# Shared down projection (last four tiles) and small attention's output projection in three float32r passes

## The chip, the cores and the metric

One core of a Trainium2 chip runs the whole kernel. The metric is device time in microseconds of that core; a kernel's figure is the median of several executions. Five engines work side by side: TensorE (PE) multiplies, its weight loads (PEld) are listed apart, VectorE (DVE), ScalarE (ACT) and GpSimd (POOL) compute on vectors, and SyncE (SP) starts the DMAs. They wait for each other by semaphores that are written out in the program.

## What is computed

Two layers on 1024 tokens of 256 features, in float32. Only the end of the second layer is touched by the change:

```python
# second layer; x: [1024, 256] tokens after its layernorm
attn = einsum('bhqk,bhkd->bhqd', probs, v)      # small attention: 16 heads of 16, over 4 positions
out  = attn @ weight_proj.T                     # [1024, 256] x [256, 256]
...
shared = silu(x @ Wsg) * (x @ Wsu) @ Wsd        # hidden width 704; Wsd: [704, 256]
shared = shared * sigmoid(x @ Wse)
...                                             # 32 experts, 4 for each token, with 32 slots each
out = shared.at[tok].add(y_pair)
x = x + attention_out + ffn_out
```

## The kernel before

The tokens are in 8 tiles of 128 (`NT`), the features in 2 chunks of 128 (`C`). `X` holds the residual, one [128, 256] block per tile. Most matmuls of the kernel are done in **three float32r passes** by `mm3` (L794 to L798): each operand is split into a high part (its copy rounded to float32r) and a low part (what is left, rounded too), and high x low, low x high and high x high are added up in one bank of PSUM. The parts are built by two engines: ACT copies the raw tensor to the high part, DVE subtracts the high part from the raw tensor. Other matmuls are plain float32.

The order of the work is written out by hand, separately for each engine. The end of the program is this:

- TensorE runs the list `EXPERT_STEPS`, in which the experts and the shared up projection take turns. The shared hidden values lie in `ACTT`, six chunks of 128 hidden rows ([128, 1024 tokens] each; the last one partly padding), raw float32. The shared down weights are `SD`, [128, 6, 256], raw, loaded long before.
- `shared_down(j)` (L1174) multiplies token tile j of the six chunks by `SD`, six float32 products of 128x128 by 128x256, into bank j % 4. Tiles 0 to 3 come first, then 16 transposes (L1202) that turn the small attention's output `AO` into banks 4 to 7, then tiles 4 to 7, each of which waits until DVE has added the tile that lay in its bank (`s_x2`).
- ACT copies the four banks of transposed heads into `AOT` (L789).
- The output stage (L1206 to L1218): for each tile, two float32 products of `AOT` with `projT`, the attention's output weights (L1214), and 16 float32r passes that take the experts' outputs `YH` and `YL` to their tokens by the masks `GT` (L1216, L1217), all in bank 4 + j % 4. From tile 4 on it waits until DVE has emptied the bank (`s_pa`).
- DVE builds the last masks (L1588), the eight low parts of the experts' outputs (`y_low`, L1592), then adds the shared tiles into `X`, scaled by the gate (`add_shared`, L1621), then the output tiles (`add_rest`, L1627). ACT builds the eight high parts of the experts' outputs (`y_high`, L758) before its four copies.
- SP stores each tile of `X` when `add_rest` is done.

Of the kernel before, what the change touches and what calls it, by code (L numbers as in the profile page):

```python
# [5 lines left out]
F32 = mybir.dt.float32  # L6
FR = mybir.dt.float32r
BF16 = mybir.dt.bfloat16
U32 = mybir.dt.uint32
ALU = mybir.AluOpType  # L10
ACT = mybir.ActivationFunctionType
AX = mybir.AxisListType.X

P = 128
B, T, D = 4, 256, 256
N = B * T
NT = N // P
C = D // P
# [25 lines left out]
FC = 6  # L44
FT = FS - P * (FC - 1)
SLOTS = E1 * CAP
GR = SLOTS // P
# [6 lines left out]
def program(nc, a, out):  # L54
    ctx = ExitStack()
    with ctx:
        def sb(name, shape, dt=F32):
            return ctx.enter_context(nc.sbuf_tensor(name, shape, dt))

        def sem(name):  # L60
            return ctx.enter_context(nc.semaphore(name))


        pb = [ctx.enter_context(nc.psum_tensor(f"bank{i}", [P, 512], F32)) for i in range(8)]
# [9 lines left out]
        at_xt = nc.sbuf_base  # L74
# [8 lines left out]
        at_wa = nc.sbuf_base  # L83
# [5 lines left out]
        at0 = nc.sbuf_base  # L89
        arena = sb("arena", [P, 35840])  # L90

        def region(at, words):
            return arena[:, at:at + words]
# [35 lines left out]
        projT = sb("projT", [P, C, D])  # L129
# [39 lines left out]
        def up_weights(g, e):  # L169
            parts = WGU[g % PLACES]  # L170
            return parts[e * len(parts) // EPG][:, e % (EPG // len(parts))]

        SGR = region(9728, 4 * FS).rearrange("p (a c n) -> p a c n", a=2, c=C)
        ACTT = [region(12800 + N * m, N) for m in range(3)] + [WAF[:, 0:N], WAF[:, N:2 * N], region(27648, N)]
# [10 lines left out]
                    (6, 0, 4, 0, 6), (7, 0, 2, 4, 6), (7, 2, 4, 0, 7)]  # L185
        SD = FRF[:, 0:1536].rearrange("p (m n) -> p m n", m=FC)
        AOT = XT
        XE = region(28672, 2048).rearrange("p (c n) -> p c n", c=C)
        SC = region(30720, 512).rearrange("p (f i h j) -> p f i h j", f=2, i=4, h=H1)
        SCf = region(30720, 512).rearrange("p (x j) -> p x j", j=4)  # L190
# [83 lines left out]
        s_ps = sem("shared_down_padding_ready")  # L274
        s_sg = sem("shared_up_weights_loaded")
        s_sd = sem("shared_down_weights_loaded")
# [16 lines left out]
        s_sm = sem("shared_product_done")  # L293
# [9 lines left out]
        s_up = sem("expert_up_done")  # L303
# [16 lines left out]
        s_ac = sem("attn1_transposed_copied")  # L320
# [12 lines left out]
        s_gt = sem("slot_masks_ready")  # L333
        s_yr = sem("expert_output_high_ready")
        s_yl = sem("expert_output_low_ready")
        s_fo = sem("attn1_projected")
        s_pa = sem("attn1_added")
        s_out = sem("out_stored")
# [33 lines left out]
        shared = [(0, 0), (1, 0), (0, 1), (1, 1)] + [(m, half) for m in range(2, FC) for half in range(2)]  # L372
# [176 lines left out]
        def _(act):  # L549
# [11 lines left out]
            for f in range(4):  # L561
                half, c = f // 2, f % 2
# [76 lines left out]
            def o_copy(u):  # L639
                _, _, b, h = unit(u)  # L640
                act.wait_ge(s_O, u + 1)
                nc.scalar.activation(QO[:, h, b], pb[4 + u % 2][:, 0:256], ACT.Identity,  # L642
                                     bias=VC[:, 32 + h:33 + h]).then_inc(s_Oc, 1)
# [103 lines left out]
            for half in range(2):  # L747
                act.wait_ge(s_di, NT)
                act.wait_ge(s_sr, 9)
                nc.scalar.activation(XE[:, 0, 512 * half:512 * half + 512], pb[4 + half][:], ACT.Copy).then_inc(s_xe, 1)  # L750
            for half in range(2):
# [4 lines left out]
            def y_high(n):  # L756
                act.wait_ge(s_ye, n + 1)
                nc.scalar.activation(YH[:, n], YE[:, n], ACT.Copy, scale=slot_w[:, n:n + 1]).then_inc(s_yr, 1)  # L758
# [25 lines left out]
                        y_high(i)  # L784
            y_high(6)
            y_high(7)
            for f in range(4):
                act.wait_ge(s_at, f + 1)
                nc.scalar.activation(AOT[:, f // 2, 512 * (f % 2):512 * (f % 2) + 512], pb[4 + f][:], ACT.Copy).then_inc(s_ac, 1)  # L789


        @block.tensor
        def _(pe):
# [92 lines left out]
            for c in range(C):  # L886
                for o in range(3):
                    ins = pe.transpose(pb[5 + c][:, P * o:P * o + P], stQKV[:, o, P * c:P * c + P], ident[:])
# [207 lines left out]
            for j in range(NT):  # L1096
                for i in range(j + 1):
                    ins = pe.matmul(pb[6][:, E1 * j:E1 * j + E1], (trib if i == j else onesb)[:], selb[:, i],
                                    start=(i == 0), stop=(i == j))
# [38 lines left out]
            def expert_up(g):  # L1138
# [8 lines left out]
                for c in range(C):  # L1147
                    for e in range(EPG):
                        s = slice(CAP * (EPG * g + e), CAP * (EPG * g + e) + CAP)
                        ins = pe.matmul(pb[4 + g % 2][CAP * e:CAP * e + CAP, 0:2 * F1], XE[:, c, s], up_weights(g, e)[:, c],  # L1150
                                        start=(c == 0), stop=(c == C - 1), skip_group_check=True)
# [22 lines left out]
            def shared_down(j):  # L1174
                if j >= 4:
                    pe.wait_ge(s_x2, j - 3)
                for m in range(FC):
                    ins = pe.matmul(pb[j % 4][:, 0:D], ACTT[m][:, P * j:P * j + P], SD[:, m], start=(m == 0), stop=(m == FC - 1))  # L1178
                ins.then_inc(s_sh, 1)

            for what, n in EXPERT_STEPS:
# [13 lines left out]
            for j in range(4):  # L1195
                shared_down(j)
            pe.wait_ge(s_ye, GR)
            pe.wait_ge(s_pv, 32)
            for f in range(4):
                c, half = f // 2, f % 2  # L1200
                for i in range(4):
                    ins = pe.transpose(pb[4 + f][:, P * i:P * i + P], AO[:, 4 * half + i, P * c:P * c + P], ident[:])  # L1202
                ins.then_inc(s_at, 1)
            for j in range(4, NT):
                shared_down(j)
            pe.wait_ge(s_ac, 4)  # L1206
            pe.wait_ge(s_gt, GR)
            pe.wait_ge(s_yl, GR)
            for j in range(NT):
                if j >= 4:  # L1210
                    pe.wait_ge(s_pa, j - 3)
                dst = pb[4 + j % 4][:, 0:D]
                for c in range(C):
                    pe.matmul(dst, AOT[:, c, P * j:P * j + P], projT[:, c], start=(c == 0), stop=False)  # L1214
                for g in range(GR):
                    pe.matmul(dst, GT[:, g, P * j:P * j + P], YH[:, g], start=False, stop=False)  # L1216
                    ins = pe.matmul(dst, GT[:, g, P * j:P * j + P], YL[:, g], start=False, stop=(g == GR - 1))  # L1217
                ins.then_inc(s_fo, 1)  # L1218
# [3 lines left out]
        def _(dve):  # L1222
# [89 lines left out]
            def chosen(k):  # L1312
                return (iota[:, None, 0:E0].to_broadcast([P, NT, E0]), topf[:, :, k:k + 1].to_broadcast([P, NT, E0]))

            for g in range(4):
# [17 lines left out]
                if g == 2:  # L1333
# [6 lines left out]
                    for k in range(2):  # L1340
                        i, t = chosen(k)
                        dst = coef if k == 0 else tmpk
# [159 lines left out]
            def shared_product(q):  # L1502
                m, half = shared[q]
                dst = ACTT[m][:, 512 * half:512 * half + 512]
                dve.wait_ge(s_ss, q + 1)
                dve.wait_ge(s_sf, 2 * q + 2)
                if m == FC - 1:
                    nc.vector.tensor_tensor(dst[P - FT:P], dst[P - FT:P], pb[up_bank(q)][P - FT:P], ALU.mult).then_inc(s_sm, 1)
                    return
                nc.vector.tensor_tensor(dst, dst, pb[up_bank(q) + 1][:], ALU.mult).then_inc(s_sm, 1)  # L1510
# [54 lines left out]
            for half in range(2):  # L1565
                dve.wait_ge(s_di, NT)
                nc.vector.tensor_copy(XE[:, 1, 512 * half:512 * half + 512], pb[6 + half][:]).then_inc(s_xd, 1)
            shared_product(3)
# [21 lines left out]
            def y_low(n):  # L1590
                dve.wait_ge(s_yr, n + 1)
                nc.vector.scalar_tensor_tensor(out=YL[:, n], in0=YE[:, n], scalar=slot_w[:, n:n + 1], in1=YH[:, n].bitcast(F32),  # L1592
                                               op0=ALU.mult, op1=ALU.subtract).then_inc(s_yl, 1)
# [25 lines left out]
            def add_shared(j):  # L1619
                dve.wait_ge(s_sh, j + 1)  # L1620
                nc.vector.scalar_tensor_tensor(out=X[:, j], in0=pb[j % 4][:, 0:D], scalar=sig[:, j:j + 1], in1=X[:, j],  # L1621
                                               op0=ALU.mult, op1=ALU.add).then_inc(s_x2, 1)
# [7 lines left out]
            slot_mask(7)  # L1630
            for n in range(GR):
                y_low(n)
            for j in range(NT):
                add_shared(j)
            for j in range(NT):
                add_rest(j)
# [23 lines left out]
```

## Time and profile before

| | |
|---|---|
| median of 3 executions | 476.18 us (475.53, 476.18, 476.19) |
| the profiled execution's own time | 475.46 us |
| its span | 473.7 us |
| PE busy | 452.1 us (95%) |
| PEld busy | 386.8 us |
| DVE busy | 287.5 us (61%) |
| ACT busy | 212.6 us (45%) |
| POOL busy | 59.9 us (13%) |

The span is the profiled time from the first instruction to the last; the execution's own time also takes in what lies around it, 1.8 us here. Busy time counts overlapping instructions once. Matmuls are pipelined, so the time from one start to the next is what a matmul costs, and its own duration is longer. A float32 product is recorded as two matmuls and two weight loads, a float32r pass as one of each.

### The profile page before, as it was taken

To read this page: it belongs to the slowest core of one execution; us is meant where nothing else is said; L and a number is where in the kernel's file an instruction comes from. 1 tells how busy PE (TensorE), PEld (TensorE's weight loads), DVE (VectorE), ACT (ScalarE), POOL (GpSimd) and SP (SyncE) were. 2 spreads that over 40 slices of the span, in tenths; PEclk is the share of its full clock that TensorE was granted. 3 is DMA by queue.
4 is the path that set the end of the run, shared out by engine and by line. 5 is a ranking of instruction groups with operands and counts; after the bars stand their busy time and mean duration, and the time that the engine had idled before them with its cause. 6 is when DMAs were issued, how large, how long until landed. Compare 5 with 4: busy or idle time off the path is not lost.

```text
span 473.7 us, 8069 instructions
## 1 busy us (share of the span) xinstructions
PE 452.1 (95%) x2934; PEld 386.8 (82%) x2934; DVE 287.5 (61%) x851; ACT 212.6 (45%) x554; POOL 59.9 (13%) x94
## 2 busy tenths in 40 slices
PE   2999999899999999999999989999998999999997
PEld 2788888698998989898989779999986755658897
DVE  5646564667676766667666555667789953545111
ACT  3454730356566566566555777233253052232000
POOL 3050000000000000000000000011345269600000
PEclk9999999999999999999999999999999999999999
DMA  6900510101000010100000000000499369910011
GB/s 202 237 28 1 178 64 26 45 1 41 5 20 27 1 46 1 46 1 0 2 1 1 1 1 1 1 1 0 172 301 292 94 166 291 309 29 2 0 46 44
DMA packets 40439, 32.32 MB, mean 68 GB/s; under 512 B 6432, under 2 KB 38864, under 8 KB 40400
## 3 DMA queue, kind: packets, MB, share of 16 engines
q1 hardware_dynamic: 40400, 31.80, 24.0%
q8 instruction: 24, 0.39, 0.3%
q14 instruction: 15, 0.12, 0.1%
HBM read 30.75 MB, written 1.05 MB: 67 GB/s over the span
## 4 chain that ended last, share of the span: by engine, by line
PE 87%; ACT 5%; DVE 4%; issue 3%; DMA 1%; POOL 0%; ACTq 0%; DVEq 0%
PE bank L796 16%; PE bank L797 15%; PE bank L798 15%; PE bank L964 5%; PE bank L946 5%; PE bank L1178 4%; PE bank L953 4%; PE bank L1109 3%; PE bank L965 3%; PE bank L945 2%; PE bank L1150 2%; PE bank L1217 2%; PE bank L1216 2%; PE bank L1214 1%; PE bank L1170 1%
## 5 line engine op out<-in xcount | busy, mean ns | idle before, releaser
L628 ACT ACTIVATE arena<-arena,nmax 128x128 f32<-128x128 f32 x64 | 25.7, 402 | 77.7 <-DVE nmax L1381 77.4
L796 PE MATMUL bank<-XTl,WA 128*128 128x512 f32 x128 | 53.9, 421 | 3.0 <-POOL WA L487 1.8
L798 PE MATMUL bank<-XTh,WA 128*128 128x512 f32 x128 | 51.2, 400 | 0.0
L797 PE MATMUL bank<-XTh,WA 128*128 128x512 f32 x128 | 51.1, 399 | 0.0
L504 POOL TENSOR_TENSOR arena<-arena 128x256 f32<-128x256 f32 x20 | 16.6, 855 | 266.1 <-ACT arena L691 247.2
L1370 DVE COPY arena<-bank 128x512 f32<-128x512 f32 x32 | 22.1, 691 | 30.7 <-PE bank L798 30.7
L964 PE MATMUL bank<-arena 128*128 128x256 f32 x128 | 39.6, 391 | 1.1 <-ACT arena L637 1.1
L1367 DVE TENSOR_SCALAR arena<-bank,VC 128x512 f32<-128x512 f32 x32 | 23.8, 748 | 24.9 <-PE bank L798 24.9
L796 PE MATMUL bank<-WA,XTh 128*128 128x256 f32 x128 | 38.3, 299 | 0.0
L946 PE MATMUL bank<-arena 128*128 128x256 f32 x128 | 38.2, 381 | 0.0
L797 PE MATMUL bank<-WA,XTl 128*128 128x256 f32 x128 | 35.8, 280 | 0.0
L798 PE MATMUL bank<-WA,XTh 128*128 128x256 f32 x128 | 35.7, 279 | 0.0
L953 PE MATMUL bank<-ident,arena 128*128 128x128 f32 x192 | 31.8, 274 | 3.2 <-DVE arena L1390 2.9
L953 PEld LDWEIGHTS bank<-ident,arena 128*128 128x128 f32 x192 | 24.3, 140 | 11.2 <-DVE arena L1390 5.6
L630 ACT ACTIVATE arena<-arena,nmax 128x256 f32<-128x256 f32 x64 | 31.6, 494 | 0.0
L796 PEld LDWEIGHTS bank<-XTl,WA 128*128 128x128 f32 x128 | 24.6, 192 | 8.5 <-POOL WA L487 2.2
L637 ACT ACTIVATE arena<-bank 128x384 f32<-128x384 f32 x64 | 30.0, 469 | 1.5 <-PE bank L953 1.5
L1414 DVE TENSOR_TENSOR OS<-arena,OS 128x1024 fp32r<-128x1024 f32 x16 | 20.1, 1267 | 16.2 <-ACT OS L660 15.8
L642 ACT ACTIVATE arena<-bank,VC 128x256 f32<-128x256 f32 x64 | 29.2, 458 | 0.3 <-PE bank L965 0.3
L798 PEld LDWEIGHTS bank<-XTh,WA 128*128 128x128 f32 x128 | 24.4, 190 | 5.8
L797 PEld LDWEIGHTS bank<-XTh,WA 128*128 128x128 f32 x128 | 24.6, 192 | 4.4
L965 PEld LDWEIGHTS bank<-arena 128*128 128x128 f32 x128 | 24.3, 190 | 3.3
(288 smaller groups left out, 1189.6 us busy)
## 6 DMA issues: line engine op xcount, KB each, us to landing
arena<-in_L_ffn_Wg SPq DMA_DIRECT2D x6, 704.0 KB, 8.5
arena<-in_L_ffn_Wu SPq DMA_DIRECT2D x6, 704.0 KB, 10.1
arena<-in_L_ffn_Wd SPq DMA_DIRECT2D x6, 512.0 KB, 8.3
arena<-in_L_attn_Wq SPq DMA_DIRECT2D x4, 512.0 KB, 6.9
arena<-in_L_attn_Wk SPq DMA_DIRECT2D x8, 256.0 KB, 2.6
arena<-in_L_attn_Wv SPq DMA_DIRECT2D x8, 256.0 KB, 3.2
arena<-in_L_attn_Wo SPq DMA_DIRECT2D x1, 2048.0 KB, 9.4
arena<-in_L_ffn_Wd SPq DMA_DIRECT2D x6, 192.0 KB, 7.7
```

The costliest lines, as they stand in the source:

```text
L628: nc.scalar.activation(Pb[i][:, 0:128], Pb[i][:, 0:128], ACT.Exp, bias=nmax[:, i, 0:1], scale=-1.0, accum_out=psumr[:, i, 0:1])
L630: nc.scalar.activation(Pb[i][:, 128:384], Pb[i][:, 128:384], ACT.Exp, bias=nmax[:, i, 1:2], scale=-1.0, accum_out=psumr[:, i, 1:2]).then_i ...
L637: nc.scalar.activation(PTb[:, u % 2], pb[2 + u % 2][:, 0:384], ACT.Copy).then_inc(s_Tc, 1)
L642: nc.scalar.activation(QO[:, h, b], pb[4 + u % 2][:, 0:256], ACT.Identity, bias=VC[:, 32 + h:33 + h]).then_inc(s_Oc, 1)
L796: pe.matmul(dst, wh, xl, start=start, stop=False)
L797: pe.matmul(dst, wl, xh, start=False, stop=False)
L798: return pe.matmul(dst, wh, xh, start=False, stop=stop)
L946: pe.matmul(s[:, 128:384], QO[:, h, b, 128:256], k[:, T * b:T * b + 256], start=True, stop=True).then_inc(s_S, 1)
L953: ins = pe.transpose(pb[2 + u % 2][:, P * i:P * i + P], Pb[u % 3][:, P * i:P * i + P], ident[:])
L964: pe.matmul(o, V[:, p % 2, 2 * b, P * hh:P * hh + P], PTb[:, u % 2, 0:256], start=True, stop=False)
L965: pe.matmul(o[:, 128:256], V[:, p % 2, 2 * b + 1, P * hh:P * hh + P], PTb[:, u % 2, 256:384], start=False, stop=True).then_inc(s_O, 1)
L1367: nc.vector.tensor_scalar(KT[:, p % 2, hh, ts], pb[6 + n % 2][:], VC[:, 16 + 2 * p + hh:17 + 2 * p + hh], None, ALU.add).then_inc(s_kc, 1)
```

## The change

It splits the second half of the shared hidden values (tokens 512 to 1023), the shared down weights, the attention's output weights and the transposed heads into high and low parts, and does the products of both projections (the shared one for tiles 4 to 7 alone) by `mm3`. ACT builds the high parts behind its last `y_high`; DVE the low parts behind its last `y_low`, with the additions of tiles 0 to 3 between them. `ACTl` is written over the raw values that it comes from; the other parts lie in memory that is free by then. Seven semaphores are added.

```diff
+        AOTh = nc.alloc_sbuf_tensor_at("AOTh", [P, C, N], FR, offset=at_xt)
+        AOTl = nc.alloc_sbuf_tensor_at("AOTl", [P, C, N], FR, offset=at0 + 4 * 17696)
+        SDh = nc.alloc_sbuf_tensor_at("SDh", [P, FC, D], FR, offset=at0 + 4 * 24576)
+        SDl = nc.alloc_sbuf_tensor_at("SDl", [P, FC, D], FR, offset=at0 + 4 * 28672)
+        ACTh = nc.alloc_sbuf_tensor_at("ACTh", [P, FC, N // 2], FR, offset=at_xt + 4 * C * N)
+        ACTl = [nc.alloc_sbuf_tensor_at(f"ACTl{m}", [P, N // 2], FR, offset=at + 4 * (N // 2))
+                for m, at in enumerate([at0 + 4 * (12800 + N * m) for m in range(3)] + [at_wa, at_wa + 4 * N, at0 + 4 * 27648])]
+        PJh, PJl = (nc.alloc_sbuf_tensor_at(f"PJ{i}", [P, C, D], FR, offset=at0 + 4 * (10240 + C * D * i)) for i in range(2))
...
@@ ACT @@
             y_high(6)
             y_high(7)
+            act.wait_ge(s_up, GR)
+            act.wait_ge(s_sd, 32)
+            act.wait_ge(s_ps, 2)
+            nc.scalar.activation(SDh[:], SD, ACT.Copy).then_inc(s_sdh, 1)
+            act.wait_ge(s_sm, len(shared))
+            for m in range(FC):
+                nc.scalar.activation(ACTh[:, m], ACTT[m][:, N // 2:N], ACT.Copy).then_inc(s_adh, 1)
+            nc.scalar.activation(PJh[:], projT[:], ACT.Copy).then_inc(s_pjh, 1)
             for f in range(4):
                 act.wait_ge(s_at, f + 1)
-                nc.scalar.activation(AOT[:, f // 2, 512 * (f % 2):512 * (f % 2) + 512], pb[4 + f][:], ACT.Copy).then_inc(s_ac, 1)
+                nc.scalar.activation(AOTh[:, f // 2, 512 * (f % 2):512 * (f % 2) + 512], pb[4 + f][:], ACT.Copy).then_inc(s_ac, 1)
@@ TensorE @@
             def shared_down(j):
                 if j >= 4:
                     pe.wait_ge(s_x2, j - 3)
+                    pe.wait_ge(s_sdl, 1)
+                    pe.wait_ge(s_adl, FC)
+                ts = slice(P * (j % 4), P * (j % 4) + P)
                 for m in range(FC):
-                    ins = pe.matmul(pb[j % 4][:, 0:D], ACTT[m][:, P * j:P * j + P], SD[:, m], start=(m == 0), stop=(m == FC - 1))
+                    if j < 4:
+                        ins = pe.matmul(pb[j % 4][:, 0:D], ACTT[m][:, P * j:P * j + P], SD[:, m], start=(m == 0), stop=(m == FC - 1))
+                    else:
+                        ins = mm3(pb[j % 4][:, 0:D], ACTh[:, m, ts], ACTl[m][:, ts], SDh[:, m], SDl[:, m], m == 0, m == FC - 1)
                 ins.then_inc(s_sh, 1)
...
             pe.wait_ge(s_ac, 4)
+            pe.wait_ge(s_al, 4)
+            pe.wait_ge(s_pjl, 1)
             pe.wait_ge(s_gt, GR)
...
                 for c in range(C):
-                    pe.matmul(dst, AOT[:, c, P * j:P * j + P], projT[:, c], start=(c == 0), stop=False)
+                    ts = slice(P * j, P * j + P)
+                    mm3(dst, AOTh[:, c, ts], AOTl[:, c, ts], PJh[:, c], PJl[:, c], c == 0, False)
@@ DVE @@
             for n in range(GR):
                 y_low(n)
-            for j in range(NT):
+            dve.wait_ge(s_sdh, 1)
+            nc.vector.tensor_tensor(SDl[:], SD, SDh[:].bitcast(F32), ALU.subtract).then_inc(s_sdl, 1)
+            for m in range(FC):
+                dve.wait_ge(s_adh, m + 1)
+                nc.vector.tensor_tensor(ACTl[m][:], ACTT[m][:, N // 2:N], ACTh[:, m].bitcast(F32), ALU.subtract).then_inc(s_adl, 1)
+                if m % 2 == 1:
+                    add_shared(m // 2)
+            dve.wait_ge(s_pjh, 1)
+            nc.vector.tensor_tensor(PJl[:], projT[:], PJh[:].bitcast(F32), ALU.subtract).then_inc(s_pjl, 1)
+            add_shared(3)
+            for f in range(4):
+                c, xs = f // 2, slice(512 * (f % 2), 512 * (f % 2) + 512)
+                dve.wait_ge(s_ac, f + 1)
+                nc.vector.tensor_tensor(AOTl[:, c, xs], pb[4 + f][:], AOTh[:, c, xs].bitcast(F32), ALU.subtract).then_inc(s_al, 1)
+            for j in range(4, NT):
                 add_shared(j)
```

Two places of the programs' instruction lists show it. The first is DVE's list behind the last low parts of the experts' outputs (`OS`), before:

```order
L1588 TENSOR_SCALAR GT<-FRF,slot_t 128x1024 x2
L1592 SCALAR_TENSOR_TENSOR OS<-arena,slot_w,YH 128x256 [waits expert_output_high_ready] x8
L1621 SCALAR_TENSOR_TENSOR X<-bank,sig,X 128x256 [waits shared_down_done] x8
L1627 TENSOR_TENSOR X<-bank,X 128x256 [waits attn1_projected,shared_added] x8
```

and in the change, where the low parts of the weights (`SDl`), of the hidden chunks (`ACTl_66` to `ACTl_71`) and of the projection weights (`PJ_73`) come between:

```order
L1624 SCALAR_TENSOR_TENSOR OS<-arena,slot_w,YH 128x256 [waits expert_output_high_ready] x8
L1666 TENSOR_TENSOR SDl<-FRF,SDh 128x1536 [waits shared_down_weights_high_ready]
L1669 TENSOR_TENSOR ACTl_66<-arena,ACTh 128x512 [waits shared_hidden_high_ready]
L1669 TENSOR_TENSOR ACTl_67<-arena,ACTh 128x512 [waits shared_hidden_high_ready]
L1653 SCALAR_TENSOR_TENSOR X<-bank,sig,X 128x256 [waits shared_down_done]
...
L1673 TENSOR_TENSOR PJ_73<-projT,PJ_72 128x512 [waits proj_high_ready]
L1653 SCALAR_TENSOR_TENSOR X<-bank,sig,X 128x256 [waits shared_down_done]
L1678 TENSOR_TENSOR AOTl<-bank,AOTh 128x512 [waits attn1_transposed_copied] x4
L1653 SCALAR_TENSOR_TENSOR X<-bank,sig,X 128x256 [waits shared_down_done] x4
L1659 TENSOR_TENSOR X<-bank,X 128x256 [waits attn1_projected,shared_added] x8
```

The eight additions that stood in one row are now spread: one behind each second hidden chunk, the fourth behind the projection weights, the other four behind the low parts of the heads.

The second place is TensorE's list at tile 4 of the shared down projection, before (`FRF` holds `SD`; the chunks are in `arena` and `WAF`):

```order
L1202 MATMUL bank<-ident,arena 128x128 x15
L1178 MATMUL bank<-FRF,arena 128x256 [waits shared_added]
L1178 MATMUL bank<-FRF,arena 128x256 x2
L1178 MATMUL bank<-FRF,WAF 128x256 x2
L1178 MATMUL bank<-FRF,arena 128x256
```

and in the change:

```order
L1231 MATMUL bank<-ident,arena 128x128 x15
L819 MATMUL bank<-SDl,ACTh 128x256 [waits shared_hidden_low_ready,shared_down_weights_low_ready,shared_added]
L820 MATMUL bank<-SDh,ACTl_66 128x256
L821 MATMUL bank<-SDh,ACTh 128x256
L819 MATMUL bank<-SDl,ACTh 128x256
L820 MATMUL bank<-SDh,ACTl_67 128x256
```

The six products of a tile have become 18 passes, and the first of them waits for all six low parts of the hidden chunks and for those of the weights.

## Rows read from the trace of the kernel before

**Rows 1.** The page: busy time by engine; granted clock in 40 slices.
```profile
PE 452.1 (95%) x2934; PEld 386.8 (82%) x2934; DVE 287.5 (61%) x851; ACT 212.6 (45%) x554; POOL 59.9 (13%) x94
...
PEclk9999999999999999999999999999999999999999
```

**Rows 2.** The chain of waits from 415 us on: start, length, what.
```profile
426.26 10.60 PE bank L1178 x48
436.86 1.75 PE bank L1202 x16
438.61 10.36 PE bank L1178 x48
448.97 0.86 PE bank L1214 x4
```

**Rows 3.** Busy time by stretch, for each engine, with granted clock and DMA.
```profile
426.26:436.69 10.43, 10.43 (x48) 9.16 (x49) 6.25 (x14) 2.45 (x7) 0.00 (x0) 1.00 0.00 1
436.69:438.44 1.75, 1.75 (x17) 1.74 (x16) 0.48 (x1) 1.11 (x3) 0.00 (x0) 1.00 0.04 9
438.44:448.80 10.36, 10.36 (x50) 9.14 (x49) 1.45 (x3) 0.96 (x2) 0.00 (x0) 1.00 0.00 0
448.80:470.94 22.14, 22.14 (x161) 21.25 (x159) 3.45 (x8) 0.00 (x0) 0.00 (x0) 1.00 0.12 42
470.94:473.70 2.76, 0.16 (x2) 0.00 (x0) 0.42 (x1) 0.00 (x0) 0.00 (x0) 1.00 0.14 48
```
The columns are the stretch and its length, then PE, PEld, DVE, ACT and POOL.

**Rows 4.** DMA issues: KB each, median us to landing; and the additions before them.
```profile
out<-X SPq DMA_DIRECT2D x8, 128.0 KB, 1.7
...
L1627 DVE TENSOR_TENSOR X<-bank,X 128x256 f32<-128x256 f32 x8 | 3.4, 424 | 18.8 <-PE bank L1217 18.8
```

**Rows 5.** Timeline of TensorE, first tile of the output stage: start, us, what.
```profile
448.80 1.03 PE L1214 MATMUL bank<-projT,XT 128*128 128x256 f32 x4
...
449.79 0.28 PE L1217 MATMUL bank<-OS,GT 128*128 128x256 f32 x1
...
451.45 0.28 PE L1217 MATMUL bank<-OS,GT 128*128 128x256 f32 x1
451.57 1.02 PE L1214 MATMUL bank<-projT,XT 128*128 128x256 f32 x4
```

**Rows 6.** Timeline of TensorE, three-pass products in the first layer's output projection.
```profile
343.25 0.28 PE L796 MATMUL bank<-FRX,OS 128*128 128x256 f32 x1
343.38 0.28 PE L797 MATMUL bank<-FRX,OS 128*128 128x256 f32 x1
343.49 0.28 PE L798 MATMUL bank<-FRX,OS 128*128 128x256 f32 x1
...
344.32 0.28 PE L796 MATMUL bank<-WA,OS 128*128 128x256 f32 x1
...
343.26 0.19 PEld L797 LDWEIGHTS bank<-FRX,OS 128*128 128x128 f32 x1
```

**Rows 7.** Timeline of ACT, from its last copies of expert outputs on.
```profile
425.42 3.30 ACT L758 ACTIVATE YH<-arena,slot_w 128x256 fp32r<-128x256 f32 x8
437.33 2.06 ACT L789 ACTIVATE XT<-bank 128x512 f32<-128x512 f32 x4 [8.62 <-PE bank L1202]
```

**Rows 8.** Groups by form: count, busy us, mean ns, idle before.
```profile
L554 ACT ACTIVATE WA<-arena 128x1024 fp32r<-128x1024 f32 x11 | 11.6, 1054 | 2.6 <-PE bank L798 2.6
L650 ACT ACTIVATE WA<-arena 128x512 fp32r<-128x512 f32 x4 | 2.5, 619 | 0.0
L1521 DVE TENSOR_TENSOR WA<-arena,WA 128x1024 fp32r<-128x1024 f32 x1 | 1.5, 1453 | 0.0
L1459 DVE TENSOR_TENSOR OS<-arena,OS 128x512 fp32r<-128x512 f32 x5 | 3.9, 781 | 0.1
```

**Rows 9.** Timeline of DVE around 431 us.
```profile
427.93 3.25 DVE L1592 SCALAR_TENSOR_TENSOR OS<-arena,slot_w,YH 128x256 fp32r<-128x256 f32 x8
431.10 1.10 DVE L1621 SCALAR_TENSOR_TENSOR X<-bank,sig,X 128x256 f32<-128x256 f32 x2
434.31 0.48 DVE L1621 SCALAR_TENSOR_TENSOR X<-bank,sig,X 128x256 f32<-128x256 f32 x1 [2.10 <-PE bank L1178]
```

**Rows 10.** Timeline of DVE in the first layer's output projection: subtractions, what follows.
```profile
330.72 1.23 DVE L1414 TENSOR_TENSOR OS<-arena,OS 128x1024 fp32r<-128x1024 f32 x1 [2.03 <-ACT OS L660]
331.86 0.41 DVE L1434 TENSOR_TENSOR XTl<-bank,XTh 128x256 fp32r<-128x256 f32 x1
...
347.10 0.69 DVE L1459 TENSOR_TENSOR OS<-arena,OS 128x512 fp32r<-128x512 f32 x1
347.71 0.42 DVE L1479 TENSOR_TENSOR X<-bank,X 128x256 f32<-128x256 f32 x1
```

More of the change, by code:

```diff
@@ L335, in program @@
         s_yl = sem("expert_output_low_ready")
+        s_sdh = sem("shared_down_weights_high_ready")
+        s_sdl = sem("shared_down_weights_low_ready")
+        s_adh = sem("shared_hidden_high_ready")
+        s_adl = sem("shared_hidden_low_ready")
+        s_pjh = sem("proj_high_ready")
+        s_pjl = sem("proj_low_ready")
+        s_al = sem("attn1_transposed_low_ready")
         s_fo = sem("attn1_projected")
```

## The prediction

> **What bounds the kernel now.** I read the page first. TensorE is busy for 95% of the span, at the full granted clock in every slice [rows 1]. A change that shortens the kernel must therefore take TensorE time out of a stretch in which TensorE is the last thing waited for. The changed stretch is the end of the program, so the chain of waits comes next [rows 2]. From 426.26 us on it runs through TensorE alone: 24 products of the shared down projection (48 records, since each float32 product is recorded twice), 16 transposes, 24 more products, and then the eight output tiles (the chain dates each piece some 0.17 us behind the start of its first record). In the table by stretches TensorE is busy for all of the last three matmul stretches, with DVE and ACT far below it: 1.45 and 0.96 us of 10.36 in the second half of the shared down projection, 3.45 and 0 of 22.14 in the output stage [rows 3]. Behind the last matmul lie 2.76 us: one DVE addition and one store, which took 1.7 us to land [rows 3, 4]. So what TensorE saves in these two stretches shortens the span one for one, if nothing new makes it wait.
>
> **The price of a float32 product.** 24 products take 10.36 us [rows 2], 0.4317 us each. I go by the distance between starts, since durations of matmuls overlap.
>
> **The price of one float32r pass.** In the output stage passes of the same 128x256 shape start at 449.79 and, 14 later, at 451.45 us: 0.1186 us apart [rows 5]. Those pairs share the token mask as weights, so I checked true three-pass code: in the first layer's output projection three consecutive passes, each with other weights, start at 343.25, 343.38 and 343.49, and nine starts after 343.25 it is 344.32: 0.1189 us each [rows 6]. I take 0.1188. Three passes are 0.356 us against 0.4317: **0.075 us saved per product**. Mixing the types costs little. Two float32 products and 16 passes add up to 0.863 + 1.901 = 2.764 us, and tiles start 2.77 us apart (448.80 and 451.57) [rows 5].
> Of the length of a pass the Trainium skill says, in "TensorE: Matmul & The Clock Gate", section "Back-to-back issue gap", that the isolated gap is N/2.4 + 2.5 ns, which makes 109 ns for 256 columns, and by that the two edits together would save 4.2 us. The trace disagrees with its 118.7 ns, and the sum goes by the trace.
>
> **Edit 1, shared down projection, tiles 4 to 7.** 24 products become 72 passes: 24 x 0.0753 = **-1.81 us**, all on the chain, if the parts are ready in time. Bounds: -2.6 us, if a pass were 0.107 us (a quarter of a float32 product), and 0, if the wait below took it all.
>
> **Edit 2, output projection.** Two products in each of eight tiles: 16 x 0.0753 = **-1.20 us**. A tile becomes 22 passes, 2.61 us. DVE's addition (0.42 us) and one 128 KB store (1.7 us) per tile still fit in that, and sit behind TensorE as before [rows 3, 4]. The banks that tiles 4 to 7 reuse need additions 0 to 3, three tiles earlier, so that wait stays empty.
>
> **Edit 3, the parts on ACT.** They are eight more copies. ACT's last copy of the expert outputs ends at 428.72, and it then waited until 437.33 for the transposes [rows 7]: 8.6 us free. A copy of 1024 columns took 1.05 us, one of 512 took 0.62 [rows 8], so 1536 columns are 1.49 us, from the difference. The high part of the weights is there at 430.2, those of the hidden tiles at 430.8 to 433.9, that of the projection at 434.5. Nothing in front is late: all these copies read things that TensorE itself needed at 426.26. Cost on the chain: nothing. The cover left before the transposes is 2.8 us; without it the same 5.8 us would stand in front of tile 4. The later copies into AOTh only change their type, and stay.
>
> **Edit 4, the parts on DVE.** DVE is free for this from 431.10 us, where the eight low parts of the expert outputs end and the additions of the shared tiles began [rows 9]; the high part of the weights (430.2) is there by then. Pitches, from one start to the next behind it: 1024 columns 1.14 us (330.72 to 331.86), 512 columns 0.61 (347.10 to 347.71) [rows 10]. 1536 columns by the difference are 1.67. Then: weights until 432.8; six hidden pieces, 3.7 us; two additions of shared tiles in between, at 0.41 us each (estimated from the 0.48 us that one of them lasts, less overlap [rows 9]), 0.8 us: the sixth piece is written at **437.3**. TensorE comes to tile 4 at 438.44 [rows 3]. The new wait is 1.1 us early, so it costs nothing.
> Queued on DVE behind these: the addition of tile 2 (437.8), the projection's low part (438.4), the addition of tile 3 (438.8), four low parts of the transposed heads (until about 441.3). Who waits: TensorE's tile 5, 6 and 7 of the shared projection need additions 1, 2 and 3, at 440.6, 442.7 and 444.9, and the output stage needs the low parts at 447.0. The nearest margin of these is nearly 5 us.
> Upper bound of this chain: the subtractions as long as those that ran beside POOL's work, end to end, 1.45 us for 1024 columns (2.18 for 1536) and 0.78 for 512 [rows 8], and 0.48 per addition. This makes 2.18 + 4.69 + 0.96 = 7.8 us, until 438.9 or, with a signal's way, 439.0: **a wait of 0.6 us**. I take none: POOL has nothing to do after 426.26 [rows 3], so the quiet rows are nearest. Below zero there is nothing, since TensorE doesn't wait there now.
>
> **The sum.** -1.81 - 1.20 + 0 = -3.01 us. Tile 4 starts at 438.44 as before, the output stage at 447.0 in place of 448.80, and the last matmul starts near 467.8. The span becomes 470.7 us, and the profiled execution 475.46 - 3.01 = 472.45. The executions shown fall in two pairs, 475.46 and 475.53, 476.18 and 476.19, so the middle of the four is 475.86, and the forecast **472.9 us**; against the median alone it would be 473.2.
>
> **Rivals.**
> *A: DVE is late for tile 4.* DVE's chain to the sixth piece takes 6.2 us by the rows and has 7.3. For: it is the longest new chain, and DVE reads there what ACT and TensorE read at the same time. Against: such reading side by side is in the stage of the first output projection too, where the passes keep their 0.119 us [rows 6]. By the upper bound it costs 0.6 us, and a chain half as long again (9.3 us) costs 2: times of 473.5 to 475. It would take 4.1 us of lateness to make the kernel slower.
> *B (the other side): the weight loads set the pace of the three passes.* Every pass brings its own load of 0.19 us [rows 6], where a float32 product had two. If a load could not run beside the pass before it here, a pass would last at least 0.19 us, a product 0.56 instead of 0.43, and 40 products cost 40 x 0.13 = +5.2 us: **481 us**. It decides from 0.144 us a pass (a third of 0.4317) on. Against it: 0.1189 us with other weights in each pass, while each load also shows 0.19 us [rows 6]. For it is only that these weights lie elsewhere in memory, and are written shortly before.
> For this rival the skill's page "TensorE: Matmul & The Clock Gate", in "The mechanism" of its part on packing, states that loads overlap running matmuls only where the row groups differ; with its 107 ns per load ("LDWEIGHTS") and 109 ns per pass a product would be three times 216, 648 ns, against 640 for the float32 product, so by that rule the change would give nothing. The trace contradicts the rule for full-width weights.
> *C: it doesn't do what it says in time*, the saving being made but given back elsewhere, as in more instructions to fetch (40 more loads and passes), or in a store that falls late. For: nothing that I see. Against: 16 passes in each of eight tiles are held at 0.119 us already [rows 5]. Time 475.2 to 476.3.
>
> **How the numbers follow.** The sum holds as told: 0.80. A, with some of the gain eaten but more than 0.95 us left: 0.08. C, or A near its end: 0.07. B or another lasting loss: 0.05. About 0.2% (0.95 us) is what a measurement of this kernel can tell from no change. So faster 0.88, same 0.07, slower 0.05. The range: low 472.2 (the lower pair's 472.45 with 0.2 more gain), high 474.2 (the median's 473.2, the bound of 0.6 us on DVE, and 0.4 of A beyond it).
>
> **What would show it.** TensorE's stretch for the second half of the shared projection 8.6 us, 72 passes 0.119 us apart, beginning at 438.4; a tile of the output stage 2.61 us; no wait of TensorE on DVE's pieces. DVE's piece of 1536 columns at 431.1, the sixth hidden piece ended near 437.3. ACT's new copies from 428.6 to 434.5. Wrong, if tile 4 starts after 438.6 (A), if passes start over 0.13 us apart (B), or if both are right and the span is yet above 471.5 (C).

## The result: 472.75 us against 475.98 us

Measured side by side, six executions each, the changed kernel's median is **472.75 us** (472.44 to 473.34), that of the kernel before 475.98 us (475.53 to 476.34). The ratio is 0.9935, with a 95% interval of 0.9922 to 0.9947: 3.1 us faster, between 2.5 and 3.7. The forecast was 472.9 us.

The profiled execution took 473.20 us, with a span of 471.5 us. From the page of the changed kernel, the busy times and the granted clock in 40 slices:

```profile
PE 450.1 (95%) x2974; PEld 386.2 (82%) x2974; DVE 295.2 (63%) x863; ACT 217.7 (46%) x562; POOL 59.9 (13%) x94
...
PEclk9999999999999999999999999999999999999999
```

Against [rows 1], TensorE has 40 matmuls more and is busy 2.0 us less; DVE and ACT have taken on 7.7 and 5.1 us. Now the same stretches as in [rows 3] (columns: stretch, length, then PE, PEld, DVE, ACT, POOL, granted clock, DMA share, GB/s):

```profile
427.16:437.59 10.43, 10.43 (x48) 9.14 (x49) 10.40 (x20) 7.47 (x15) 0.00 (x0) 1.00 0.00 1
437.59:439.34 1.75, 1.75 (x18) 1.75 (x16) 1.75 (x4) 1.11 (x3) 0.00 (x0) 1.00 0.00 0
439.34:447.77 8.43, 8.43 (x75) 8.43 (x73) 3.95 (x8) 0.96 (x2) 0.00 (x0) 1.00 0.01 2
447.77:468.71 20.94, 20.94 (x178) 20.87 (x176) 3.46 (x8) 0.00 (x0) 0.00 (x0) 1.00 0.13 45
468.71:471.50 2.79, 0.13 (x2) 0.00 (x0) 0.42 (x1) 0.00 (x0) 0.00 (x0) 1.00 0.13 47
```

Both tables begin at the first product of tile 0. The first two stretches have their old length, and the last is 0.03 us longer. The second half of the shared projection went from 10.36 to 8.43 us (-1.93), the output stage from 22.14 to 20.94 (-1.20). TensorE is busy through all of both. DVE is now busy for 10.40 of the 10.43 us in which the float32 tiles run: that is where the parts are built. The timelines of DVE and ACT in the changed kernel answer to [rows 7, 9]:

```profile
428.83 3.25 DVE L1624 SCALAR_TENSOR_TENSOR OS<-arena,slot_w,YH 128x256 fp32r<-128x256 f32 x8
432.00 1.75 DVE L1666 TENSOR_TENSOR SDl<-FRF,SDh 128x1536 fp32r<-128x1536 f32 x1
433.66 1.29 DVE L1669 TENSOR_TENSOR ACTl<-arena,ACTh 128x512 fp32r<-128x512 f32 x2
...
437.45 0.69 DVE L1669 TENSOR_TENSOR ACTl<-arena,ACTh 128x512 fp32r<-128x512 f32 x1
438.06 0.49 DVE L1653 SCALAR_TENSOR_TENSOR X<-bank,sig,X 128x256 f32<-128x256 f32 x1
...
439.44 2.48 DVE L1678 TENSOR_TENSOR AOTl<-bank,AOTh 128x512 fp32r<-128x512 f32 x4
```

```profile
429.52 1.47 ACT L805 ACTIVATE SDh<-FRF 128x1536 fp32r<-128x1536 f32 x1
...
434.02 0.62 ACT L809 ACTIVATE PJ<-projT 128x512 fp32r<-128x512 f32 x1
```

The sixth hidden piece ends at 437.45 + 0.69 = 438.14 us. The first pass of tile 4 follows the transposes without a gap, 1.12 us later (timeline of TensorE):

```profile
439.26 0.36 PE L819 MATMUL bank<-SDl,ACTh 128*128 128x256 f32 x1
439.46 0.28 PE L820 MATMUL bank<-SDh,ACTl 128*128 128x256 f32 x1
```

All times in this trace are 0.90 us later than in the kernel before, already at 427.16 against 426.26. The last section tells where these 0.90 us come from; they are not made by the change. So below I compare **the end part**, from the first product of tile 0 to the end of the span: 473.7 - 426.26 = 47.44 us before, 471.5 - 427.16 = 44.34 us after, **-3.10 us**.

### The profile page after: what moved, and what is told of

Same layout as the page of the kernel before. It is cut to its first block, busy times and chain, and to the rows that moved or that the text cites. A ratio compares the mean times of both kernels' runs of the same rounds, so it can differ in the third digit from the quotient of the medians.

```text
span 471.5 us, 8175 instructions
## 1 busy us (share of the span) xinstructions
PE 450.1 (95%) x2974; PEld 386.2 (82%) x2974; DVE 295.2 (63%) x863; ACT 217.7 (46%) x562; POOL 59.9 (13%) x94
## 4 chain that ended last, share of the span: by engine, by line
PE 87%; ACT 5%; DVE 4%; issue 3%; DMA 1%; POOL 0%; ACTq 0%; DVEq 0%
PE bank L819 17%; PE bank L820 17%; PE bank L821 17%; PE bank L987 5%; PE bank L969 5%; PE bank L976 4%; PE bank L1132 3%; PE bank L988 3%; PE bank L968 2%; PE bank L1205 2%; PE bank L1173 2%; PE bank L1249 2%; PE bank L1248 2%; PE bank L1193 1%; PE bank L1019 1%
```

## Each half of the change alone

Run e1 does the shared projection as the change does, and leaves the output projection as it was:

```diff
-            nc.scalar.activation(PJh[:], projT[:], ACT.Copy).then_inc(s_pjh, 1)
...
-            pe.wait_ge(s_al, 4)
-            pe.wait_ge(s_pjl, 1)
...
-                    mm3(dst, AOTh[:, c, ts], AOTl[:, c, ts], PJh[:, c], PJl[:, c], c == 0, False)
+                    pe.matmul(dst, AOT[:, c, P * j:P * j + P], projT[:, c], start=(c == 0), stop=False)
```

> The change to the shared down projection alone; the output projection stays in float32, without its parts. Theory (each float32 product saves 0.075 us of TensorE time, and nothing waits): the second half of the shared projection lasts 8.4 to 8.6 us instead of 10.36, a tile of the output stage 2.77 as before; time 1.8 to 1.9 us below the kernel before, near 474.1. Rival C (a saving is given back elsewhere): both parts of the change are needed together, or this one alone gives under 1 us.

Run e2 does the reverse:

```diff
-                    if j < 4:
-                        ins = pe.matmul(pb[j % 4][:, 0:D], ACTT[m][:, P * j:P * j + P], SD[:, m], start=(m == 0), stop=(m == FC - 1))
-                    else:
-                        ins = mm3(pb[j % 4][:, 0:D], ACTh[:, m, ts], ACTl[m][:, ts], SDh[:, m], SDl[:, m], m == 0, m == FC - 1)
+                    ins = pe.matmul(pb[j % 4][:, 0:D], ACTT[m][:, P * j:P * j + P], SD[:, m], start=(m == 0), stop=(m == FC - 1))
```

> The change to the output projection alone; the shared projection stays in float32, without its parts. Theory: a tile of the output stage lasts 2.61 us instead of 2.77, the shared projection 10.36 as before; time 1.2 us below the kernel before, near 474.8, and the two halves add up to what the whole change gives (3.0 to 3.2). Rival C: stores or additions at the end bound the output stage, and the gain is under 0.6 us.

| | ratio to before, 95% interval | median | end part | against before |
|---|---|---|---|---|
| e1, shared alone | 0.9959 (0.9944 to 0.9974) | 474.34 | 472.9 - 427.36 = 45.54 | -1.90 |
| e2, output alone | 0.9976 (0.9966 to 0.9987) | 475.13 | 472.7 - 426.44 = 46.26 | -1.18 |
| the change | 0.9935 (0.9922 to 0.9947) | 472.75 | 44.34 | -3.10 |

The kernel before had 476.15 us beside e1 and e2. The same stretches in e1, then in e2:

```profile
439.54:447.97 8.43, 8.43 (x74) 8.43 (x73) 1.45 (x3) 0.95 (x2) 0.00 (x0) 1.00 0.00 0
447.97:470.10 22.13, 22.13 (x162) 21.25 (x160) 3.45 (x8) 0.00 (x0) 0.00 (x0) 1.00 0.12 42
```

```profile
438.62:448.98 10.36, 10.36 (x51) 9.13 (x49) 3.45 (x7) 0.95 (x2) 0.00 (x0) 1.00 0.00 0
448.98:469.90 20.92, 20.92 (x177) 20.86 (x175) 3.45 (x8) 0.00 (x0) 0.00 (x0) 1.00 0.13 45
```

Each half shortens its own stretch and leaves the other alone, and 1.90 + 1.18 = 3.08 is the whole but for 0.02. Nothing is given back (rival C falls).

## How early DVE is, and what a wait costs

Runs e3 and e6 make DVE late on purpose: the low part of the weights is computed again, two times more in e3, once more in e6.

```diff
+            for i in range(2):
+                step(nc.vector.tensor_tensor(SDl[:], SD, SDh[:].bitcast(F32), ALU.subtract))
             nc.vector.tensor_tensor(SDl[:], SD, SDh[:].bitcast(F32), ALU.subtract).then_inc(s_sdl, 1)
```

> The changed kernel with the low part of the shared down weights computed three times instead of once, each waiting for the one before: DVE's chain in front of tile 4 is some 3.7 us longer (two times 1.75 us and a step between). In the changed kernel the sixth hidden piece ended 1.2 us before TensorE came to tile 4. Theory: TensorE waits for 3.7 - 1.2 = 2.5 us before tile 4, the time rises by the same 2.5 us to about 475.2, so the margin is real and one for one beyond it. If the margin were only apparent (rival A: TensorE already waits for DVE in some hidden way), the time would rise by the full 3.7 us, to 476.5; if DVE were not on any path, by nothing.

e3 took 477.11 us in its one execution. Its end part is 475.4 - 426.88 = 48.52 us, **4.18 us** more than the changed kernel's 44.34, where 2.5 was expected. The trace of e3 has the wait itself, and more (timeline of TensorE):

```profile
441.60 0.36 PE L819 MATMUL bank<-SDl,ACTh 128*128 128x256 f32 x1 [2.37 <-DVE ACTl L1671]
...
442.71 0.41 PE L819 MATMUL bank<-SDl,ACTh 128*128 128x256 f32 x1
442.93 0.41 PE L820 MATMUL bank<-SDh,ACTl 128*128 128x256 f32 x1
...
445.81 0.28 PE L820 MATMUL bank<-SDh,ACTl 128*128 128x256 f32 x1
445.93 0.28 PE L821 MATMUL bank<-SDh,ACTh 128*128 128x256 f32 x1
```

and the table by stretches of e3, whose PEclk column is the third from the end:

```profile
439.00:441.40 2.40, 0.23 (x3) 0.00 (x0) 2.40 (x6) 1.02 (x3) 0.00 (x0) 1.00 0.00 0
441.40:443.00 1.60, 1.40 (x8) 1.43 (x9) 1.60 (x5) 0.00 (x0) 0.00 (x0) 0.68 0.04 10
443.00:445.00 2.00, 2.00 (x11) 2.00 (x11) 2.00 (x4) 0.00 (x0) 0.00 (x0) 0.50 0.00 0
445.00:447.00 2.00, 2.00 (x18) 2.00 (x17) 0.72 (x2) 0.00 (x0) 0.00 (x0) 0.90 0.00 0
```

After TensorE had done the 16 transposes and then stood still for 2.37 us, its granted clock went to 0.50, the lower of its two levels (1.2 of 2.4 GHz), while it was already working again; the trace has it so from 441.97 to 445.38 us. Between 442.07 and 445.27 us 15 passes take 0.213 us each where they would take 0.117, which is 1.4 us, and with the passes at either edge about 1.6. Tile 4 begins 14.72 us behind the first product of tile 0 (426.88 to 441.60) and 12.10 us behind it in the changed kernel (427.16 to 439.26): it is 2.6 us late, and with 1.6 us of half clock this is the 4.18. All this is one execution. In the same execution TensorE also waited for 1.6 us near 363 us, and the clock stayed at 1.00 there. Whether a wait of 2.4 us would bring the half clock at any other place, and not only behind the transposes, no run shows.

> The changed kernel with the low part of the shared down weights computed twice: DVE's chain is 1.8 us longer, TensorE's wait before tile 4 about 1.8 - 1.2 = 0.6 us. With two extra subtractions the wait was 2.37 us and TensorE's granted clock was at half for some 3.3 us after it, which cost 1.6 us more. Theory 1 (a short wait is one for one): passes 0.117 us apart right behind the wait, granted clock 1.0, time 0.6 us above the changed kernel. Theory 2 (any wait here brings the half clock): a stretch with passes 0.21 us apart behind it, time 1.5 to 2.3 us above.

e6 asks whether a short wait at this place does the same. It does not. The timeline of TensorE in e6, and the stretch behind the wait:

```profile
439.08 0.36 PE L819 MATMUL bank<-SDl,ACTh 128*128 128x256 f32 x1 [0.58 <-DVE ACTl L1670]
439.27 0.28 PE L820 MATMUL bank<-SDh,ACTl 128*128 128x256 f32 x1
```

```profile
439.40:441.00 1.60, 1.60 (x16) 1.60 (x15) 1.60 (x4) 0.00 (x0) 0.00 (x0) 1.00 0.04 10
```

The wait is 0.58 us, the clock stays at 1.00, the passes at 0.117. The end part is 471.3 - 426.15 = 45.15 us, 0.81 more than the changed kernel, and tile 4 begins 0.83 us late (426.15 to 439.08 is 12.93 us, against 12.10). So this delay reaches the end one for one. (The idle time in brackets counts from the recorded end of the last transpose and is 0.25 us shorter than the delay, in e3 too.) The two executions took 472.98 and 473.05 us, only 0.2 to 0.3 above the median of the changed kernel beside them (472.78); the profiled one (473.05) had reached tile 0 early, at 426.15 us, and the last section tells why that varies.

How much of the 1.12 us is real margin? The sixth hidden piece in e3 and in e6 (timelines of DVE):

```profile
440.77 0.68 DVE L1671 TENSOR_TENSOR ACTl<-arena,ACTh 128x512 fp32r<-128x512 f32 x1
```

```profile
438.25 0.68 DVE L1670 TENSOR_TENSOR ACTl<-arena,ACTh 128x512 fp32r<-128x512 f32 x1
```

In both runs TensorE starts 0.15 us behind its end (441.45 to 441.60, and 438.93 to 439.08): this is the way of the signal and TensorE's restart. So the margin is 1.12 - 0.15 = 0.97 us. The delays agree with it: DVE's chain is 1.80 us longer in e6 and TensorE 0.83 late, 3.59 us longer in e3 and TensorE 2.62 late.

## How short a pass can get

Run e4 cuts each of the 72 passes into two of 128 columns:

```diff
-                for m in range(FC):
...
+                for h in range(2):
+                    hs = slice(P * h, P * h + P)
+                    for m in range(FC):
+                        if j >= 4:
+                            ins = mm3(pb[j % 4][:, hs], ACTh[:, m, ts], ACTl[m][:, ts], SDh[:, m, hs], SDl[:, m, hs], m == 0, m == FC - 1)
```

> The changed kernel with each of the 72 passes of the shared projection's tiles 4 to 7 done as two passes of 128 columns, so 144 passes and 144 weight loads for the same result. Theory (the loads run beside the passes, and a pass costs its columns plus some 10 ns): 0.064 us a pass, the stretch 9.2 us instead of 8.4, time 0.8 us above the changed kernel. Rival B, in its weak form (a load has its own pace, hidden only behind a wide pass): with a floor of 0.107 to 0.12 us per load the stretch lasts 15.4 to 17 us, time 7 to 9 us above the changed kernel. Rival B in its strong form (0.19 us per load, in turn): 27 us, 19 us above.

The result was 480.38 us in one execution, and the end part 478.7 - 426.70 = 52.00 us, 7.66 more than the changed kernel. My theory (0.8 more) fell, and the 7 to 9 more of the weak form of rival B came true. The timeline of TensorE and its weight loads in e4:

```profile
439.39 0.27 PE L821 MATMUL bank<-SDh,ACTh 128*128 128x128 f32 x1
439.44 0.19 PEld L819 LDWEIGHTS bank<-SDl,ACTh 128*128 128x128 f32 x1
439.50 0.28 PE L819 MATMUL bank<-SDl,ACTh 128*128 128x128 f32 x1
439.56 0.19 PEld L820 LDWEIGHTS bank<-SDh,ACTl 128*128 128x128 f32 x1
439.62 0.27 PE L820 MATMUL bank<-SDh,ACTl 128*128 128x128 f32 x1
```

Passes start 0.112 us apart: the 144 take 16.1 us, and half the columns bought 4% per pass. This floor lies just under the 0.117 us of the 256-column pass. e4 alone does not tell whether the load makes it or a fixed cost of a pass, since each pass has one load. The trace of the kernel before has more streams in which every pass has its own load: float32 passes of only 16 columns, float32 transposes of 65 rows and 65 columns, and bfloat16 passes of 32 columns (TensorE and its weight loads, three places):

```profile
40.29 0.82 PE L830 MATMUL bank<-R2T,arena 128*128 128x16 f32 x6
40.38 0.64 PEld L830 LDWEIGHTS bank<-R2T,arena 128*128 128x128 f32 x5
```

```profile
384.43 0.54 PE L1135 MATMUL bank<-ident,arena 65*128 65x65 f32 x6
```

```profile
358.51 0.18 PE L1098 MATMUL bank<-selb,onesb 128*128 128x32 bf16 x1
358.51 0.10 PEld L1098 LDWEIGHTS bank<-selb,trib 128*128 128x128 bf16 x1
358.53 0.18 PE L1098 MATMUL bank<-selb,trib 128*128 128x32 bf16 x1
```

A single pass of the first kind is recorded with 0.26 us, so six in 0.82 us start 0.11 us apart, although they have an eighth of e4's columns. A single transpose is recorded with 0.23 us, so those start 0.06 us apart, and the bfloat16 passes 0.025. So the columns do not make the floor, and neither does a fixed cost of every pass or of every float32 pass. What is left is the load of 128x128 weights of four bytes; no run changes that load alone.

The loads also overlap the passes: in the page "TensorE: Matmul & The Clock Gate" of the Trainium skill a load of 128 columns takes 107 ns (section "LDWEIGHTS"), close to this floor, while a load and a 128-column pass in turn would take 107 + 53 = 160 ns by its figures, an estimate. The rule that a load overlaps running matmuls only where the row groups differ, in the section "The mechanism" of this page of the Trainium skill, does not hold for these full-width weights. The same section also says that a load is pulled ahead if it goes to the background weight buffer, and with that the 0.112 us agree.

## A version that beats both

By the measured prices another tile costs DVE little and saves TensorE 0.48 us. Run e5 does tiles 2 to 7 in three passes. For that, the parts must be ready earlier:

```diff
+        FIRST = 2
+        LATER = N - P * FIRST
...
-            for n in range(GR):
-                y_low(n)
             dve.wait_ge(s_sdh, 1)
...
+            add_shared(0)
+            add_shared(1)
+            slot_mask(6)
+            slot_mask(7)
+            for n in range(GR):
+                y_low(n)
+            add_shared(2)
+            add_shared(3)
...
-                    pe.wait_ge(s_adl, FC)
...
+                        pe.wait_ge(s_adl, m + 1)
```

> A further step: tiles 2 to 7 of the shared projection in three passes (12 more products), the transposes moved up behind tile 1, and on ACT and DVE the parts of the shared projection moved ahead of the experts' output parts, the last two masks and the additions; tile 2 waits chunk by chunk. By the pitches of the changed kernel (0.4317 us a float32 product, 0.117 a pass, so 0.081 us saved per product): tiles 0 and 1 end at 426.3 + 5.2, the transposes at 433.2, tiles 2 to 7 at 445.8 us instead of 446.9; DVE's last hidden piece is ready at 434.0 and needed at 434.9, the low parts of the heads at 443.1 and needed at 445.8. Theory: 1.0 us below the changed kernel, near 471.8. Rival A: DVE falls behind tile 2 or behind the output stage; then TensorE waits, and as the run with two extra subtractions showed, a wait of over 2 us brings a stretch of half clock behind it, so the time would be above that of the changed kernel.

> The changed kernel itself once more, on the same chip and beside the same runs of the kernel before as the version with six tiles, for a direct comparison: 2.9 to 3.3 us below the kernel before.

| | ratio to before (476.23 beside them), 95% interval | median | end part |
|---|---|---|---|
| e5, six tiles | 0.9910 (0.9896 to 0.9924) | 471.69 (471.62 to 472.12) | 469.8 - 426.34 = 43.46 |
| e7, the change again | 0.9936 (0.9922 to 0.9950) | 472.78 (472.61 to 473.62) | 470.9 - 426.57 = 44.33 |

e5 is 1.1 us faster by the medians, the slowest of its five executions (472.12) is below the fastest of the changed kernel's eleven (472.44), and the end part is 0.87 us shorter, where 1.0 was expected. Here DVE runs just ahead of TensorE (timelines of both in e5):

```profile
433.26 0.36 PE L820 MATMUL bank<-SDl,ACTh 128*128 128x256 f32 x1
...
435.10 0.28 PE L820 MATMUL bank<-SDl,ACTh 128*128 128x256 f32 x1
...
446.04 0.28 PE L820 MATMUL bank<-PJ,AOTh 128*128 128x256 f32 x1
```

```profile
433.03 0.95 DVE L1667 TENSOR_TENSOR ACTl<-arena,ACTh 128x768 fp32r<-128x768 f32 x1
...
440.56 2.48 DVE L1681 TENSOR_TENSOR AOTl<-bank,AOTh 128x512 fp32r<-128x512 f32 x4
```

The last hidden piece ends at 433.98 us, 0.7 us *behind* the start of tile 2, and its product is the last of the tile, from 435.10 us on. TensorE has no wait there, since it waits for one chunk at a time. The low parts of the heads end at 443.04 and are needed at 446.04.

## Why the prediction was right, step by step

- **TensorE bounds this part.** Shown: what its two stretches lost (1.93 + 1.20), less 0.03 us that the tail is longer, is the change of the end part (3.10).
- **The float32 product, 0.4317 us.** Unchanged in e2: 24 in 10.36 us.
- **The float32r pass, 0.1188 us.** Too high by a little in the shared projection: 72 in 8.43 us, 0.1171 each. In the output stage 176 take 20.94 us, 0.1190. The 109 ns of the formula in the Trainium skill ("TensorE: Matmul & The Clock Gate", section "Back-to-back issue gap") would have promised 4.2 us; the trace's own pitch was the right one to take.
- **Edit 1**: -1.81 forecast, -1.93 measured. **Edit 2**: -1.20 forecast, -1.20 measured, with a tile of 2.61 us (e2: 451.59 to 454.21). The small error of edit 1 is the pass.
- **Edit 3 (ACT)**: copies of 1.47 and 0.62 us against 1.49 and 0.62 forecast, the last of them ended at 434.64 us, 3.6 us before ACT's next task at 438.23. Hidden, as forecast. I had added up durations; the copies of 512 columns start 0.52 us apart, so the eight were done some 0.8 us sooner than the 434.5 forecast, once the 0.90 us are taken off.
- **Edit 4 (DVE)**: the sixth piece came 6.14 us after DVE was free (432.00 to 438.14), against 6.2 forecast, and 1.12 us before tile 4, against 1.1. The upper bound of 0.6 us of wait was not needed. Of the 1.12 us, 0.15 are the way of the signal, which the sum left out.
- **Rival A** was priced wrongly. I took lateness as one for one. It is so for a wait of 0.58 us (e6), but a wait of 2.37 us cost 1.6 us more in half clock (e3). The 4.1 us of lateness from which the change was to lose are the margin of 1.1 and the gain of 3.0. In e3 DVE's chain is only 3.6 us longer, and its end part of 48.52 us is already above the 47.44 of the kernel before; in e6 it is 1.8 us longer, and 45.15 us is still a gain. Where between the two it turns, no run shows. My sign for A, a tile 4 that starts after 438.6, was badly chosen: it does start at 439.26, but it would have had to be measured from the first product of tile 0.
- **Rival B**: the threshold was 0.144 us a pass, and the floor that e4 shows is 0.112. The rival was wrong for 256 columns, and right that there is a floor: in passes of 128 columns the same product costs six times 0.112, 0.67 us, and loses to the 0.43 of float32. The 640 and 648 ns that I compared there by figures of the Trainium skill are both far off: the float32 product takes 432 ns and three passes 351.
- **What I said would show C**, a span above 471.5 with both stretches right, nearly came true (471.5, where 470.7 was forecast) and meant nothing of the kind: the 0.8 us arose at the start of the kernel, as the last section shows. That the forecast came within 0.15 us of the median is partly luck. The gain was 3.2 us between the medians and not 3.0, the middle that I started from (475.86) was 0.1 us below the median measured beside the change (475.98), and my forecast for a profiled execution, 472.45, was 0.75 us below the 473.20 that it took. What the runs bear out is the end part, -3.10 us against -3.01.

## What to carry to other kernels

Price a change of number format by the distance between starts of passes with the same width that reload their weights, not by durations or formulas; at 128x256 three float32r passes cost 0.35 us and a float32 product 0.43, but cut into passes of 128 columns they cost 0.67. Put the building of the parts where vector engines idle in front of float32 work that is kept as cover, measure the margin by making the helper late, and let the consumer wait piece by piece. Leave a margin on such a helper: in e3 a wait of TensorE of 2.37 us was paid once as a wait and again, with 1.6 us, as half clock.

## What the runs showed of the hardware that I had not expected

**The half clock behind a wait.** As shown with e3, in one execution: 16 transposes, 2.37 us without matmuls, then 0.50 granted up to 445.38 us, at a cost of 1.6 us; after the transposes and 0.58 us, nothing.

**The scatter of the profiled executions comes from the start.** The first 512-column passes of every profiled execution start 0.427 us apart, then, from some point on, 0.233. In the timeline of TensorE before, the pace changes at 13.4 us, in the changed kernel at 15.4 us; first before, then after:

```profile
13.01 0.63 PE L798 MATMUL bank<-XTh,WA 128*128 128x512 f32 x1
13.43 0.53 PE L796 MATMUL bank<-XTl,WA 128*128 128x512 f32 x1
13.80 0.39 PE L797 MATMUL bank<-XTh,WA 128*128 128x512 f32 x1
```

```profile
14.95 0.63 PE L820 MATMUL bank<-XTh,WA 128*128 128x512 f32 x1
15.38 0.52 PE L821 MATMUL bank<-XTh,WA 128*128 128x512 f32 x1
15.74 0.39 PE L819 MATMUL bank<-XTl,WA 128*128 128x512 f32 x1
```

512 columns in 0.427 us is the pace of 1.2 GHz, yet the granted clock reads 1.00 in this stretch in both traces. The reading is empty: the traces have no record of the clock before 13.72 us (before) and 15.64 us (changed). There the first one begins, with full clock, in the very interval in which the pace changes. Before these passes TensorE had stood idle for 6.7 us, done a few transposes and waited 1.8 us more (6.6 and 1.7 in the changed kernel).

There are 5 slow intervals before and 10 after. Five more at 0.194 us are 0.97 us, less the 0.18 us by which the first pass came earlier: 0.79 of the 0.90 us that the changed kernel is behind at 427 us. The code of this stretch is the same in all runs, and their traces fit:

| | first record of full clock, us | first product of tile 0, us |
|---|---|---|
| before (first pass 0.18 us later than in the change) | 13.72 | 426.26 |
| e6 | 13.73 | 426.15 |
| e5 | 14.05 | 426.34 |
| e7 | 14.55 | 426.57 |
| e4 | 14.79 | 426.70 |
| e3 | 15.30 | 426.88 |
| the change | 15.64 | 427.16 |
| e1 | 16.11 | 427.36 |

The trace of e2 has no record of the clock. Each microsecond of later rise costs about half a microsecond: with half of the time from the first pass to the rise taken off, the first product of tile 0 comes 414.0 to 414.1 us behind the first pass in all eight. The change and e7 are the same kernel, and differ there by 0.59 us, as do their times (473.20 and 472.61). That the executions without a trace scatter for the same reason is likely, and not shown. What moves the rise was not tried.
